# Metaformer block: a one-product second bias, epsilon columns, top-2 from logits, and written-out orders for the first and last images

## The reference

```
x = x + attention(ln_c(x))            # q (8 heads of 16), k, v (16 each); softmax of k over tokens, of q over its 16
t = tokens(x)
x = x + moe0(ln_t(t))                 # router on the image's mean: 2 of 8 experts per image, 64->128->64, exact gelu,
                                      # weights by a second softmax; then layer norm of (mixture + input), gamma, beta
x = x + conv3x3(ln_c(x))              # weights are scale * sign(w), scale = mean |w| per output channel
x = x + moe1(ln_t(tokens(x)))         # router per token: softmax of 8 logits, the two largest probabilities are the
                                      # gates, experts 64->128->64 with exact gelu, biases b1 and b2
```

## Time and profile before

| | |
|---|---|
| median of 3 runs | 394.39 us |
| the profiled execution | 394.83 us |
| its span, first to last instruction | 393.0 us |
| PE busy | 333.8 us, 85% |
| DVE busy | 279.6 us, 71% |
| ACT busy | 233.6 us, 59% |
| POOL busy | 93.0 us, 24% |
| mean granted TensorE clock | 0.927 |
| attention stage | to 109.9 us |
| router | to 119.1 us |
| images | to the end |

### The profile page before, as it was taken

One profiled execution on the slowest core, in us unless ns is written; L12 is line 12 of the kernel. 1 busy time (PEld: TensorE's weight loads), 2 busy tenths in 40 slices (PEclk: granted clock), 3 DMA queues, 4 the chain that ended last, 5 costly groups with the idle time before them and its releaser, 6 DMA issues.

```text
span 393.0 us, 5235 instructions
## 1 busy us (share of the span) xinstructions
PE 333.8 (85%) x1719; PEld 179.1 (46%) x1719; DVE 279.6 (71%) x586; ACT 233.6 (59%) x440; POOL 93.0 (24%) x76
## 2 busy tenths in 40 slices
PE   3868999999817155889999999999999999898695
PEld 3457787878702042443444344244344344234131
DVE  2495989899550515739969869969969969974571
ACT  2433858686634315665956957858858766656531
POOL 4323464654500202203103103103103103102000
PEclk9978999999966658599999999999999999999968
DMA  5951000000000000047067075085083093191491
GB/s 148 165 157 32 1 3 2 0 3 2 2 0 0 0 2 1 1 136 296 0 189 269 1 235 224 0 275 185 3 329 128 5 344 110 38 373 49 118 339 28
DMA packets 25835, 41.17 MB, mean 105 GB/s; under 512 B 15376, under 2 KB 16144, under 8 KB 25808
## 3 DMA queue, kind: packets, MB, share of 16 engines
q1 hardware_dynamic: 25808, 40.83, 32.9%
HBM read 38.47 MB, written 2.36 MB: 104 GB/s over the span
## 4 chain that ended last, share of the span: by engine, by line
PE 45%; DVE 17%; ACT 13%; issue 10%; SPq 6%; DMA 5%; POOL 2%; POOLq 1%; ACTq 0%; DVEq 0%
PE ps L696 14%; PE ps L807 9%; PE ps L742 5%; PE ps L712 3%; ACT HB L1395 3%; DMA GB<-spread 3%; SPq L411 2%; POOL rstdA L457 2%; DVE qsum L969 2%; ACT L1382 2%; ACT L1395 2%; PE ps L727 2%; DVE HB L1191 1%; PE ps L621 1%; ACT XN L1355 1%
## 5 line engine op out<-in xcount | busy, mean ns | idle before, releaser
L696 PE MATMUL ps<-ET,W1B 64*128 64x512 f32 x256 | 70.2, 652 | 2.4 <-ACT HB L1395 1.9
L1191 DVE TENSOR_TENSOR HB<-HB,GB 128x1024 f32<-128x1024 f32 x44 | 53.2, 1222 | 21.6 <-DMA GB<-spread 21.1
L1395 ACT ACTIVATE HB<-ps,B1B 128x1024 f32<-128x1024 f32 x44 | 47.4, 1112 | 9.6 <-PE ps L696 9.2
L807 PE MATMUL ps<-HB,W2B 128*64 128x512 f32 x176 | 47.5, 630 | 3.7 <-DVE HB L1191 3.7
L457 POOL TENSOR_TENSOR rstdA<-varA,pow_half 128x8 f32<-128x8 f32 x16 | 28.8, 1802 | 74.3 <-DVE varA L891 74.3
L457 POOL TENSOR_TENSOR rstdB<-varB,pow_half 128x8 f32<-128x8 f32 x8 | 14.0, 1749 | 130.4 <-DVE varB L891 130.4
L696 PEld LDWEIGHTS ps<-ET,W1B 64*128 64x128 f32 x256 | 21.5, 193 | 45.8 <-issue 25.2
L457 POOL TENSOR_TENSOR rstd<-var,pow_half 128x4 f32<-128x4 f32 (+1 forms) x24 | 29.1, 1217 | 32.6 <-DVE var L891 31.9
L742 PE MATMUL ps<-VP,WC 128*128 128x512 f32 x96 | 28.4, 450 | 1.4 <-ACT VP L1363 1.4
L1191 DVE TENSOR_TENSOR XC<-XC,GB 128x1024 f32<-128x1024 f32 x20 | 24.2, 1221 | 7.3 <-DMA GB<-spread 7.3
L742 PEld LDWEIGHTS ps<-VP,WC 128*128 128x128 f32 x96 | 19.3, 208 | 11.9 <-ACT VP L1363 6.6
(11 more groups left out here) (215 smaller groups left out, 651.1 us busy)
## 6 DMA issues: line engine op xcount, KB each, us to landing
GB<-spread SPq DMA_DIRECT2D x64, 512.0 KB, 7.8
out<-W1stage SPq DMA_DIRECT2D x8, 256.0 KB, 3.7
XC<-in_x SPq DMA_DIRECT2D x6, 256.0 KB, 5.7
T<-in_x SPq DMA_DIRECT2D x1, 512.0 KB, 3.7
W1A<-in_w1a SPq DMA_DIRECT2D x1, 512.0 KB
W1B<-in_w1b SPq DMA_DIRECT2D x1, 512.0 KB
W1stage<-in_wconv SPq DMA_DIRECT2D x1, 288.0 KB, 3.0
W1stage<-in_wcs SPq DMA_DIRECT2D x1, 288.0 KB, 2.9
```

The lines of the kernel that those rows point to most:

```text
L696: mm(ps[:, H_BANKS[n % 2][c], :], weights[half(c), :], tokens(half(c)), start=True, stop=True).then_inc(s["h"], 1)
L807: ins = mm(acc(b)[c * C:(c + 1) * C, :], W2B[:, e, :], HG[b][e][:, c * HALF:(c + 1) * HALF], start=False, stop=(e == E - 1), skip_group_ch ...
L1191: tt(HG[b][e], HG[b][e], GB[:, e, :], ALU.mult).then_inc(s["f_hg"], 1)
L1395: av(HG[b][e], HID[n % 2], ACT.Gelu, bias=B1B[:, e:e + 1]).then_inc(s["gelu"], 1)
```

## The change

1. **Second bias.** `f_bias` is one fp32r product of 512 columns. Its moving operand G3R holds the gates as rows (8 experts x 2 halves, times three groups at partitions 0, 32 and 64): the rounded gates, the rest that rounding left, and the rounded gates again; its stationary operand B2R holds b2 rounded, b2 rounded, and b2's rest. The rows come from `spread` in six loads of 16 KB behind GB's eight; POOL rounds them and makes the rest (`b_rows`). B2F takes six small loads where B2X took eight.
2. **Epsilon columns.** The squares are scaled by 1/8 before squaring and are written between two constant columns that hold the epsilons; the sum over 65 columns is the variance. The 48 variance steps of line 891 are gone. SQA has its own tile, CV lies in its old place.
3. **Top-2 from logits.** `b_first` and `b_second` work on the logits less their maximum; `b_exp` writes elsewhere, and `b_probs` comes after `b_second`. CW = (first + second) * exp * 1/sum. 14 steps, not 16.
4. **Banks.** Image 1's first mixture uses the second accumulator's bank (bank 7), so `a_output` of image 1 waits only for the router and that of image 2 only for the two copies of image 0.
5. **Orders.** For images 2 to 5 a new `PLAN`; the start and the end are lists of their own (`FIRST`, `LAST`). In `FIRST` the first mixtures of images 1 and 2 are ahead of image 0's experts. `ATTENTION_PLAN` is new too.

```diff
-        for layer, k, ahead in RING:
+        for layer, k, ahead in sorted(RING) if b == 0 else RING:
...
     pool=(
-        "b_rstd-1 a_rstd0 a_rstd1"
+        "b_rows-1 a_rstd1+1 b_rstd+1 a_rstd0+2"
...
+    assert sorted(parts) == sorted(part for part, _ in parts_of(PLAN[name]))
+    in_order(FIRST[name])
+    for b in STEADY:
+        period(b, b % 2, PLAN[name], parts, image_exists)
+    in_order(LAST[name])
...
+        def a_bank(b):
+
+            return ACC_BANK[1] if b == 1 else A_BANK
...
+                sp.wait_ge(s["b_g3"], 2 * b + 1)
+                for group in range(3):
+                    for h in range(2):
+                        row = 32 * group + E * h
+                        sp.dma_start(G3[row:row + E, :], spread[b, :, h * HALF:(h + 1) * HALF]).then_inc(s["spread_rows"], 16)
...
+            def b_rows(b, par):
+                pool.wait_ge(s["spread_rows"], 6 * 16 * (b + 1))
+                ge(pool, s["f_bias"], b)
+                pool.tensor_copy(G3R[:, :], G3).then_inc(s["b_g3"], 1)
+                pool.wait_ge(s["b_g3"], 2 * b + 2)
+                pool.tensor_tensor(G3R[32:48, :], G3[32:48, :], f32(G3R[32:48, :]), ALU.subtract).then_inc(s["b_g3"], 1)
+                pool.wait_ge(s["b_g3"], 2 * b + 3)
...
-                ge(pe, s["a_img"], 2 * b)
+                if b == 1:
+                    pe.wait_ge(s["router_dve"], RD_B2)
+                else:
+                    ge(pe, s["a_img"], 2 if b == 2 else 2 * b)
...
-                pe.wait_ge(s["b_cwt"], b + 1)
-                for j in range(4):
-                    ins = mm(acc(b)[:, j * P:(j + 1) * P], B2X[:, j, :], GT[:, par, :], start=False, stop=False,
-                             skip_group_check=True)
-                ins.then_inc(s["f_bias"], 1)
+                pe.wait_ge(s["b_g3"], 2 * b + 3)
+                mm(acc(b), B2R[:, :], G3R[:, :], start=False, stop=False, skip_group_check=True).then_inc(s["f_bias"], 1)
...
-                    vr(ssA[:, :], SQA[:, :, :], X, ALU.add).then_inc(s["a_ss"], 1)
-                    variance(ssA[:, :], varA[:, :], (LN_T_EPS, LN_C_EPS)[k], 2 * b + k + 1, "a_ss", "a_var")
+                    vr(varA[:, :], SQA[:, :, (SUM_T, SUM_C)[k]], X, ALU.add).then_inc(s["a_var"], 1)
...
-                    av(SQA[:, :, :], (ZA, XA)[k][:, :, :], ACT.Square).then_inc(s["a_sq"], 1)
+                    av(SQA[:, :, 1:C + 1], (ZA, XA)[k][:, :, :], ACT.Square, scale=ROOT).then_inc(s["a_sq"], 1)
...
-                av(G[:, 1], G[:, 1], ACT.Exp).then_inc(s["b_exp"], 1)
+                av(G[:, 2], G[:, 1], ACT.Exp).then_inc(s["b_exp"], 1)
```

More of the change, by code:

```diff
@@ new lines @@
+        "square1_1+2 set_fold+2 query_exp2+1 query_channels1+1 u_channels2 channels1_0+2 residual0+1 channels1_1+2 "
+        "query_exp3+1 keys_values0+2 residual1+1 keys_values1+2 set_outputs+2 query_channels2+1 key_exp+2 "
+        "query_exp0+2 tokens_kv+2 set_second-2 query_exp1+2 u_channels3"
+    ).split(),
+)
+FIRST = dict(
+    pool=(
+        "a_rstd0:0 a_rstd1:0 a_rstd0:1 b_rstd:0 a_rstd1:1 a_rstd0:2 b_rstd:1 b_rows:0 a_rstd1:2 b_rstd:2 a_rstd0:3"
+    ).split(),
+    pe=(
[8 rows of a table added]
+    ).split(),
+    vec=(
[8 rows of a table added]
+    ).split(),
+    act=(
[6 rows of a table added]
+    ).split(),
+)
@@ L139 @@
+LAST = dict(
+    pool=(
+        "b_rows:5 a_rstd1:7 b_rstd:7 b_rows:6 b_rows:7"
+    ).split(),
+    pe=(
[7 rows of a table added]
+    ).split(),
+    vec=(
+        "b_residual:7 b_centre:7 b_ss:7 b_normalise:7 f_gated2:6 f_gated3:6 b_logits:7 b_first:7 b_second:7 "
+        "b_probs:7 b_weights:7 f_gated4:6 f_gated5:6 f_gated6:6 f_gated7:6 f_gated0:7 f_gated1:7 f_gated2:7 "
+        "f_gated3:7 f_gated4:7 f_gated5:7 f_gated6:7 f_gated7:7"
+    ).split(),
+    act=(
[4 rows of a table added]
     ).split(),
@@ L141 @@
 MOST_AHEAD = 2
+STEADY = range(2, 6)
+B_TOP = 14
+LOWEST = -3.0e38
 def parts_of(plan):
@@ L155, in period, with periods, in_order @@
             parts[name](b + ahead, (par + ahead) % 2)
-def periods(plan, parts):
+def periods(name, parts):
     def image_exists(name, b, ahead):
         return 0 <= b + ahead < B
-    assert sorted(parts) == sorted(name for name, _ in parts_of(plan))
-    for b in range(-MOST_AHEAD, B + MOST_AHEAD):
-        period(b, b % 2, plan, parts, image_exists)
+    def in_order(tokens):
+        for token in tokens:
+            part, b = token.split(":")
+            parts[part](int(b), int(b) % 2)
+    assert sorted(parts) == sorted(part for part, _ in parts_of(PLAN[name]))
[3 more added lines that the diff above has]
+    in_order(LAST[name])
 def pair_periods(name, parts):
@@ L317, in build @@
         HA = XC[:, 0:2, :]
-        ZA, SQA, ZN, ZG = (tiles(XN[:, k // 2, (k % 2) * HALF:(k % 2 + 1) * HALF]) for k in range(4))
-        ssA = sb("ssA", [P, TILES])
+        ZA, ZN, ZG = (tiles(XN[:, k // 2, (k % 2) * HALF:(k % 2 + 1) * HALF]) for k in (0, 2, 3))
+        SQA = sb("SQA", [P, TILES, C + 2])
         varA = sb("varA", [P, TILES])
@@ L978, in part @@
                     vec.wait_ge(s["sq2"], n + 1)
[L979 to L980 removed]
+                    if n == 0:
+                        vec.wait_ge(s["memsets"], EPS_SET)
+                    vr(var2[:, n % 2, :], SQ2[:, n % 2, :, SUM_T], X, ALU.add).then_inc(s["var2"], 1)
                 return part
@@ L1156, in b_logits, with b_first @@
                 steps.done(tt(G[:, 1], G[:, 0], gv[:, 0, :].unsqueeze(2).broadcast_to([P, TILES, E]), ALU.subtract))
+            def b_first(b, par):
+                vec.wait_ge(s["b_lg"], 3 * b + 3)
+                steps = steps_of(vec, s["b_top"], B_TOP * b)
+                wide = [P, TILES, E]
+                steps.done(vec.scalar_tensor_tensor(G[:, 3], G[:, 1], 0.0, rev.unsqueeze(1).broadcast_to(wide),
+                                                    ALU.is_equal, ALU.mult))
+                steps.wait()
+                steps.done(vr(gq[:, 0, :], G[:, 3], X, ALU.max))
+                steps.wait()
+                steps.done(tt(G[:, 5], G[:, 3], gq[:, 0, :].unsqueeze(2).broadcast_to(wide), ALU.is_equal))
+                steps.wait()
+                steps.done(vec.scalar_tensor_tensor(G[:, 6], G[:, 5], LOWEST, G[:, 1], ALU.mult, ALU.add))
+                assert steps.n == 4
```

181 lines of the change are left out of this document (91 added, 90 removed), and 41 rows, old and new, of tables (act, pe, vec).

## The result

The changed kernel took 384.36 us (median of 4; 383.77 to 384.91) against 394.66 for the kernel before (median of 4; 393.87 to 395.58): a ratio of 0.976, with an interval of 0.973 to 0.978. It is faster, but the gain is 10.3 us of the 25.5 forecast, and the time lies above the range, whose high end was 380. The profiled execution took 384.80 us for a span of 383.0.

What follows compares the result with a forecast made beforehand. TensorE's products were taken to bound the steady part, neither TensorE nor VectorE alone attention. Start and attention -6.1, filling -11.4, steady -3.0, emptying -5.0 summed to -25.5 from 394.83, giving 369 us; range 362 to 380.

Steps and rivals of the forecast that it cites:

- Steady part, -3.0 forecast: Convolution 2 to 6: the cheaper bias product saves about 0.75 us per image, over four images -3.0 us.
- so both lie beside other work: Steady part: six row loads on SyncE and POOL's cast and product, about 1 us each, run beside other work.
- my first rival: POOL's two row operations hold up VectorE's products of SBUF operands: +9.6 us over six images, 378.6 us; chance 0.25.
- Emptying, -5.0 forecast: Convolution 6 to the last product: the last order takes 68.0 us where it took 73.0, so -5.0 us.
- Start and attention, -6.1 forecast: Up to the first mixture: loads -1.4, pairs -4.2 and the last pair's end -0.5, together -6.1 us.
- I take 1.4, three times: Attention: dropped variance steps and new order save 1.4 us per pair, between bounds of 0 and 2.0.
- attention gains nothing beyond the loads: Rival: TensorE bounds attention, so only the loads help: +4.7 us, 374 us; chance 0.08.
- The term of the loads, 1.4: Start: six small bias loads, not eight, and set_conv ahead of query_max2 save 1.4 us together.
- Filling, -11.4 forecast: Image pipeline's start: the third convolution starts at 190.2, not 201.63, so -11.4 us.
- gating can start at 168.6: Filling: CW's copy stands ahead of a gelu on ScalarE, so gating starts at 168.6, not 175.72 us.
- I take the full clock, -2.1: Filling: with products on both sides of the old gap, image 0's convolution runs at full clock, saving 2.1 us.
- The slower rival (rows late): Row loads land late and images wait: 4.2 us each over six images, 395 us and more; chance 0.05 with the like.

Runs made afterwards that it cites:

- experiment 12: Changed kernel with row operations in idle stretches and bias products of images 0, 5 and 6 later: 375.52 us; with 24 unread extra products, 375.01 us.
- 9: Changed kernel with POOL's row operations of images 0 to 6 waiting for the last gated product, bias products of images 5, 6 later: 381.10 us; second set 379.42.
- 2: Changed kernel with POOL's cast and product touching 8 of 512 columns from image 1 on: 376.73 us, ratio 0.957 to the kernel before.
- experiment 7: Changed kernel with the explicit first order taken away, image 1's mixture in the common bank, experts' buffers in the steady turn: 391.61 us, ratio 0.994.
- after: The profile of the changed kernel itself: profiled execution 384.80 us for a span of 383.0.
- experiment 11: The kernel of 9 plus 24 unread products, 11 in the router's gap and 13 ahead of image 0's token turning: 378.85 us, ratio 0.961.

## Why the prediction was wrong

The sum was 15.5 us too low for the profiled execution. The largest part is the collision of POOL's rows with VectorE, which the sum put at nothing: without it (experiment 12, no extra products) the median is 8.8 us lower. By TensorE's marks that is 1.5 us in the filling, 4.8 in the steady part and 2.8 in the emptying, of which half clock is 1.4. That version also has the bias products of images 0, 5 and 6 later. By its steps:

- **Steady part, -3.0 forecast, +2.5 measured.** The failed step is "so both lie beside other work". They lay beside work, but in VectorE's way, which was my first rival, at 0.25. Its mechanism and its place (the products behind a_zn) were right, and its price nearly: 1.33 us an image, not 1.6. The path was not quite right: the first wait that TensorE sees is not CW but gelu 0, by way of the square. Of both kinds of row the wide product was the nearer one; I let the power of 8 columns speak against it. But the step of 0.85 us in that row has one SBUF operand, and the products held here have two, so the row was near and not the same. The bias was sized nearly right, 0.66 for 0.75, though one product costs 0.43 to the next group and not 0.27. With the collision my sum would have been 378.6, inside the range but still 5.8 us below the measured time.
- **Emptying, -5.0 forecast, -0.8 measured.** The failed term is the same one: the rows have no price here either. Without the hold it is -3.6 to -4.1 (experiments 9 and 2), or -2.0 where a stretch of lower clock falls into it (the second trace of 9). In this execution such a stretch of half clock took some 1.5 us.
- **Start and attention, -6.1 forecast, -3.5 measured.** The failed term is "I take 1.4, three times". I read 20.25 of 20.38 us of TensorE as inflated by waits inside streams; it was the bound (20.1 to 20.2 in the old orders and the new). The rival "attention gains nothing beyond the loads" was right for the pairs: 0.15 each. Yet the columns are needed, since the new orders with the step take 21.0. The term of the loads, 1.4, was too small, and that was luck: the queue's time for them fell from 4.91 to 2.02 us, VectorE had the second load 3.1 us earlier (30.97 for 34.05), and with the old loads the stage would have lost 1.1 us against before, not gained 3.5. The gain is not a sum of terms: the old loads cost 4.6 us, the old step 3.5, the old orders 3.2, each alone against the change.
- **Filling, -11.4 forecast, -8.2 measured.** From the first mixture product, gates started 2.3 us earlier (3.1 forecast), CW ended 5.2 (6.1), the first gated product 3.9 (7.1), and the stretch from there to convolution 2 took 21.65 us (21.6 forecast). The failed step is "gating can start at 168.6": from CW's end I allowed 7.0 us; it took 9.3: 1.9 to the copy of the turned matrix on ScalarE (160.89), of which 1.2 for the two hidden products at half clock ahead of the turning, and 7.4 from there (6.4 in the earlier trace rows). I had asked what the clock does to the convolution, and not what it does to the gates after it. For the convolution itself the answer was wrong too: "I take the full clock, -2.1" brought 0.8 (4.54 us for 5.32), and a shorter way from its end to the gates (8.8 us, 9.7 forecast) hid most of that. The agreement of 21.65 with 21.6 is luck as well: 1.24 of it is the wait for image 1's CW, and without the collision the stretch took 20.2 us (168.19 to 188.39, experiment 12). That the order carries the stage was right (experiment 7).

The slower rival (rows late) cost nothing that a trace shows. In the steady part the rows were there when POOL came to them. In the filling POOL stood 5.17 us for image 0's rows with `a_rstd1` of image 2 behind them, but TensorE did not wait for what hangs on that norm.

## What to carry to other kernels

Work that is moved to POOL is not free when it is small: look which VectorE instructions run at its new moment, those with two SBUF operands above all and in the start and the end too, and give it a semaphore that starts it where VectorE waits anyway. Where an engine's order is fixed, a later producer must be followed by moving its consumer as well; variants here lost 12 and 2 us to one product left where it stood. When an engine is busy 99% of a period, take that as the bound first, and ask for a reason before calling the time inflated.

## What the runs showed of the hardware

- A POOL instruction 512 columns wide holds VectorE products of two SBUF operands, which end 0.55 us after it (1.07 and 1.64 us for 0.69), and also one of 64 columns (1.04 for 0.22). It is held by them too: POOL's own difference took 1.59 us there and 1.27 alone.
- Narrow POOL instructions did not hold VectorE. The cast of 8 columns took 0.18 us; the difference of 8 columns took 0.56 beside VectorE's product and 0.20 away from it, and both products stayed at 0.69. The power of 8 columns took 2.01 and 2.48 us where VectorE's product with two SBUF operands had begun just before it (259.04, 268.12), and 1.64 at 256.75, where the product came later; it held none of them. Why it does not is not shown.
- Six loads into 8 neighbouring partitions each took 2.02 us of SyncE's queue, 0.34 each; eight loads of the same table into every eighth partition took 4.90 us, 0.61 each.
- After TensorE had stood for most of 106 to 113.6 us, it was at the lower level (1.2 GHz) until about 122 us in after. The 11 products put into that gap did not change this in a way that can be told: the first two groups of hidden products behind it took 2.82 and 1.99 us in one version with them (experiment 11), 3.54 and 3.08 in the other (12), and from 3.50 to 3.79 and from 1.99 to 3.79 in traces without them.
- With the same waits of TensorE in front (2.3 and 0.6 us), the clock fell to the lower level for some 3.6 us in one execution of the changed kernel (330.2 to 333.8 us, mean 0.52) and stayed at full in another.
